# A fused recurrent and mixture-of-experts layer on 8 cores: the order of its tail and of its last weight loads

## The reference, cut to what matters

```
xn = layernorm(x)                                # x: 2 x 8192 tokens x 1024
h_t = sigmoid(A) * h_(t-1) + xn_t @ B            # 64 states, scan over time
s  = h @ C + xn @ D
r  = sigmoid(xn @ gate_w + gate_b)               # 16 experts, the best 2 per token
mlp(x, wg, wu, wd) = (silu(x @ wg) * (x @ wu)) @ wd      # 1024 -> 512 -> 1024
moe = w1 * mlp(xn, expert_1) + w2 * mlp(xn, expert_2)    # w1 + w2 = 1
out = x + s * silu(xn + mlp(xn, shared) + moe)
```

## Time and profile before

| | us |
|---|---|
| median of 3 timed runs | 740.28 (739.29 to 740.67) |
| the profiled execution | 733.69 |
| span of its slowest core (core 6) | 732.1 |
| spans of the 8 cores | 721.0 to 732.1 |
| PE / VectorE / ScalarE / GpSimd busy on the page's core (span 731.9) | 454.5 / 245.6 / 176.1 / 163.6 |

### The profile page before, as it was taken

How to read it: one execution, slowest core, us unless ns; L and a number is a source line. 1 busy time by engine, 2 the same in 40 slices (tenths; PEclk the granted TensorE clock), 3 DMA queues, 4 the chain that set the end, 5 groups by cost and what they waited for, 6 DMA issues and landing times.

```text
span 731.9 us, 7940 instructions; the slowest of 8 cores (721.0 to 732.1 us)
## 1 busy us (share of the span) xinstructions
PE 454.5 (62%) x2742; PEld 246.0 (34%) x2776; DVE 245.6 (34%) x437; ACT 176.1 (24%) x242; POOL 163.6 (22%) x167
## 2 busy tenths in 40 slices
PE   0126649965995484782872975838838787874530
PEld 0123324433552252450540543515514333331210
DVE  3763533472211121120210211201202567772235
ACT  0233321301322131320320321313203132221111
POOL 2110110022332132141230331412202123231113
PEclk9999968999999698797896997988979899997785
DMA  8971129401999999999999999999997565663421
GB/s 191 235 249 58 45 100 159 87 27 56 154 179 198 186 213 173 194 199 199 183 194 203 189 164 204 199 190 165 197 207 213 191 220 197 217 213 124 169 109 57
DMA packets 29705, 122.71 MB, mean 168 GB/s; under 512 B 5277, under 2 KB 5661, under 8 KB 22880
## 3 DMA queue, kind: packets, MB, share of 16 engines
q0 software_dynamic: 17136, 81.15, 58.7%
q1 hardware_dynamic: 12528, 41.03, 16.3%
HBM read 150.87 MB, written 33.55 MB: 252 GB/s over the span
## 4 chain that ended last, share of the span: by engine, by line
DMA 33%; PE 31%; DVE 14%; ACT 7%; issue 6%; DVEq 4%; POOL 2%; POOLq 1%; SPq 0%; ACTq 0%
DMA y_dram<-ysb,pidx 25%; PE ps L764 10%; PE ps L378 8%; PE ps L382 8%; DVEq L79 4%; DVE xgT L1085 4%; DVE xgT L1088 3%; DMA x_sb<-x_in 2%; ACT ysb L1091 2%; ACT xgT L1053 2%; DMA xn_dram<-xgT 2%; DMA a_t<-adiag 2%; PE ps L722 1%; POOL ysb L1095 1%; PE ps L466 1%
## 5 line engine op out<-in xcount | busy, mean ns | idle before, releaser
L764 PE MATMUL ps<-ring,xgT 128*128 128x512 bf16 (+1 forms) x368 | 101.0, 414 | 115.2 <-ACT ysb L775 89.3
L777 DVE COPY ysb<-ps 128x512 f32<-128x512 f32 (+1 forms) x48 | 33.1, 691 | 206.5 <-DMA y_dram<-ysb,pidx 120.9
L764 PEld LDWEIGHTS ps<-ring,xgT 128*128 128x128 bf16 (+1 forms) x384 | 36.7, 109 | 174.7 <-issue 152.0
L378 PE MATMUL ps<-xgT,ring 128*128 128x320 bf16 x512 | 82.2, 304 | 8.4 <-ACT silu L392 7.0
L382 PE MATMUL ps<-xgT,ring 128*128 128x320 bf16 x512 | 80.3, 300 | 0.0
L775 ACT ACTIVATE ysb<-ps 128x512 f32<-128x512 f32 (+1 forms) x48 | 28.6, 595 | 206.4 <-DMA y_dram<-ysb,pidx 135.2
L392 ACT ACTIVATE silu<-ps 128x320 f32<-128x320 f32 (+1 forms) x80 | 37.6, 470 | 136.2 <-PE ps L382 135.9
L399 DVE TENSOR_TENSOR xgT<-silu,ps 128x320 bf16<-128x320 f32 x64 | 31.2, 488 | 115.2 <-ACT silu L392 115.2
L1069 PE MATMUL ps<-ring,xnT 128*128 128x512 bf16 x252 | 67.2, 412 | 2.1 <-DVE ysb L1093 1.9
L1095 POOL TENSOR_TENSOR ysb<-ysb,x_sb 128x1024 f32<-128x1024 f32 x16 | 38.7, 2417 | 125.0 <-DVE ysb L1093 125.0
L378 PEld LDWEIGHTS ps<-xgT,ring 128*128 128x128 bf16 x512 | 48.5, 99 | 32.7 <-issue 14.5
(11 more groups left out here) (130 smaller groups left out, 471.1 us busy)
## 6 DMA issues: line engine op xcount, KB each, us to landing
ring<-ewg POOLq DMA_DIRECT2D x16, 1024.0 KB
ring<-ewu POOLq DMA_DIRECT2D x16, 1024.0 KB, 24.9
ring<-ewd POOLq DMA_DIRECT2D x16, 1024.0 KB, 23.6
ring<-y_dram SPq DMA_DIRECT2D x32, 512.0 KB, 5.4
x_sb<-x_in SPq DMA_DIRECT2D x16, 512.0 KB, 25.7
out<-ysb SPq DMA_DIRECT2D x16, 512.0 KB, 3.0
xn_dram<-xgT SPq DMA_DIRECT2D x16, 256.0 KB, 3.2
ysb<-x_in SPq DMA_DIRECT2D x6, 512.0 KB, 7.4
```

Of the source, the lines that this page charges most:

```text
L378: PE.op(lambda e, c=c: e.matmul(bank(p)[:, 0:n], slot_gu(m, c, ic), rhs(c), start=(c == 0), stop=(c == 7)))
L764: f = lambda q, k=k, h=h, dst=dst: q.matmul(dst, inter(e, k, o, n), slot_d(m, k, h), start=(k == 0), stop=(k == 3))
L777: k2 = V.sig(lambda q, to=to, src=src: q.tensor_copy(to, src))
```

## The change

The order of things changes in five places. The number of instructions of each kind and the bytes moved stay the same.

1. Loads 47, 48, 49 are now the shared down and D's halves; loads 50, 51, 52 are expert 15's gate, up and down. The `y_load` buffers move with them. When each numbered load is issued stays as it was.
2. `tail_front(0)` and the first sum of tile 0 stand between expert 15's gate and up and its down.
3. The first sum is taken out of `tail_front` (`tail_sum`); that of tile t+1 now stands between fma2 and the product of tile t.
4. x of tiles 12 to 15 is asked for in `tail_back(t)`, t = 0 to 3, right behind the write of tile t.
5. The part for overfull experts uses other PSUM banks and another buffer; it has nothing to do here.

```diff
+            if m >= M_SD and m < M_SD + 3:
+                return (swd, dmat[0], dmat[1])[m - M_SD]
+            e, j = divmod(m - 2, 3) if m < M_SD else (E - 1, m - M_SD - 3)
+            return (ewg, ewu, ewd)[j][e]
-        M_SD = 2 + 3 * E
+        M_SD = 2 + 3 * (E - 1)
+        def m_of(e):
+            return 2 + 3 * e if e < E - 1 else M_SD + 3
...
         for e in range(E):
-            m = 2 + 3 * e
+            m = m_of(e)
...
             for mm in (m + 6, m + 7):
-                if mm < M_SD + 3:
+                if mm < M_SD + 6:
                     load_w(mm)
...
+            if e == E - 1:
+                PE.wait(FREE_G[0], FREE_G[1], FREE_U[0], FREE_U[1], prev_scan[0],
+                        T_W[M_SD], T_W[M_D0], T_W[M_D1], *[T_MUL[("s", g)] for g in range(16)])
+                A.wait(FREE_XGT[e])
+                tail_front(0)
+                tail_sum(0)
             PE.wait(T_W[m + 2], *[T_MUL[(e, ic)] for ic in range(4)])
...
         def tail_front(t):
             b = 4 * (t % 2)
-            if t >= NXR:
-                s = t - NXR
-                SP.wait(T_F[s])
-                T_XR[t] = SP.dma(lambda e: e.dma_start(out=x_fin(t), in_=x_rows(t)), s_xr[s])
-            A.wait(T_XR.get(t), T_S.get(t - 2), LASTPE, T_DV)
+            A.wait(T_XR.get(t), T_S.get(t - 2))
...
-            V.wait(T_AN[t], T_P1[t])
-            T_A1[t] = V.sig(lambda e: e.tensor_tensor(ab[t % 2], ab[t % 2], bank(b, 2), ALU.add))
+        def tail_sum(t):
+            V.wait(T_AN[t], T_P1[t])
+            T_A1[t] = V.sig(lambda e: e.tensor_tensor(ab[t % 2], ab[t % 2], bank(4 * (t % 2), 2), ALU.add))
...
         def tail_back(t):
...
             T_S[t] = A.sig(lambda e: e.activation(g, a, AF.Silu))
+            if t + 1 < NT:
+                tail_sum(t + 1)
             V.wait(T_S[t], T_P2[t])
             T_H[t] = V.sig(lambda e: e.tensor_tensor(g, g, bank(b + 2, 2), ALU.mult))
...
             T_O[t] = SP.dma(lambda e: e.dma_start(out=out[t * 128:(t + 1) * 128, :], in_=g), s_o[t % 3])
+            if t + NXR < NT:
+                T_XR[t + NXR] = SP.dma(lambda e: e.dma_start(out=x_fin(t + NXR), in_=x_rows(t + NXR)), s_xr[t])
...
         for t in range(2):
             T_YF[t] = y_load(t)
-        tail_front(0)
+        PE.wait(T_DV, T_DA)
```

More of the change, by code:

```diff
@@ L753, in down_tile @@
         def down_tile(e, j, o, p0, n):
-            m = 4 + 3 * e
+            m = m_of(e) + 2
             yb = j % NYB
@@ L801, in build_nc, with x_fin @@
             FREE_Y[b] = R["inv"]
+        M_D0, M_D1 = M_SD + 1, M_SD + 2
+        XW = [slot(m_of(E - 1) + i) for i in range(3)]
+        yf = [w.bitcast(F32) for w in XW]
+        ab = [xgT[:, i * 2048:(i + 1) * 2048].bitcast(F32) for i in range(2)]
+        gb = [ysb[:, i * D:(i + 1) * D] for i in range(3)]
+        T_AN, T_P1, T_P2, T_A1, T_A2, T_A3, T_S, T_H, T_O, T_F = ({} for _ in range(10))
+        T_YF, T_XR = {}, {}
+        def x_fin(t):
+            s = t if t < NXR else t - NXR
+            return x_sb[:, s * D:(s + 1) * D]
@@ new lines, in y_load @@
+        def y_load(t):
+            SP.wait(T_DONE, *LASTG)
+            if t >= 3:
+                SP.wait(T_A3[t - 3])
+            SP.dma(lambda e: e.dma_start(out=yf[t % 3][:, 0:D],
+                                         in_=y_dram[t * 128:(t + 1) * 128, :]), s_yf[t % 3])
+            return SP.dma(lambda e: e.dma_start(out=yf[t % 3][:, D:2 * D],
+                                                in_=y_dram[T_OWN + t * 128:T_OWN + (t + 1) * 128, :]),
+                          s_yf[t % 3])
@@ new lines, in tail_front @@
+        def tail_front(t):
+            b = 4 * (t % 2)
+            A.wait(T_XR.get(t), T_S.get(t - 2))
+            T_AN[t] = A.sig(lambda e: e.activation(ab[t % 2], x_fin(t), AF.Identity,
+                                                   bias=nmr[:, t:t + 1], scale=rstd[:, t:t + 1]))
+            PE.wait(T_A1.get(t - 2))
+            for h in range(2):
+                for k in range(4):
+                    f = lambda e, h=h, k=k: e.matmul(bank(b + h), interS[:, k * T_OWN + t * 128:k * T_OWN + (t + 1) * 128],
+                                                     slot_d(M_SD, k, h), start=(k == 0), stop=(k == 3))
+                    if (h, k) == (1, 3):
+                        T_P1[t] = PE.sig(f)
+                    else:
+                        PE.op(f)
+            PE.wait(T_H.get(t - 2))
+            for h in range(2):
+                PE.op(lambda e, h=h: e.matmul(bank(b + 2 + h), hs[:, HALO + t * 128:HALO + (t + 1) * 128],
+                                              csb[:, h * 512:(h + 1) * 512], start=True, stop=False))
+                for c in range(8):
+                    f = lambda e, h=h, c=c: e.matmul(
+                        bank(b + 2 + h), xnT[:, c * T_OWN + t * 128:c * T_OWN + (t + 1) * 128],
+                        slot_d(M_D0 if c < 4 else M_D1, c % 4, h), start=False, stop=(c == 7))
+                    if (h, c) == (1, 7):
+                        T_P2[t] = PE.sig(f)
+                    else:
+                        PE.op(f)
@@ new lines, in tail_sum, with tail_back @@
+        def tail_sum(t):
+            V.wait(T_AN[t], T_P1[t])
+            T_A1[t] = V.sig(lambda e: e.tensor_tensor(ab[t % 2], ab[t % 2], bank(4 * (t % 2), 2), ALU.add))
+        def tail_back(t):
+            b = 4 * (t % 2)
+            a = ab[t % 2]
+            g = gb[t % 3]
+            V.wait(T_YF[t], R["w"])
+            V.drain()
+            V.op(lambda e: e.scalar_tensor_tensor(a, yf[t % 3][:, 0:D], wts[:, t:t + 1], a,
+                                                  ALU.mult, ALU.add))
+            V.drain()
+            T_A3[t] = V.sig(lambda e: e.scalar_tensor_tensor(a, yf[t % 3][:, D:2 * D], wts[:, NT + t:NT + t + 1],
+                                                             a, ALU.mult, ALU.add))
+            A.wait(T_A3[t], T_O.get(t - 3))
+            T_S[t] = A.sig(lambda e: e.activation(g, a, AF.Silu))
+            if t + 1 < NT:
+                tail_sum(t + 1)
+            V.wait(T_S[t], T_P2[t])
+            T_H[t] = V.sig(lambda e: e.tensor_tensor(g, g, bank(b + 2, 2), ALU.mult))
+            G.wait(T_H[t])
+            T_F[t] = G.sig(lambda e: e.tensor_tensor(g, g, x_fin(t), ALU.add))
+            SP.wait(T_F[t])
+            T_O[t] = SP.dma(lambda e: e.dma_start(out=out[t * 128:(t + 1) * 128, :], in_=g), s_o[t % 3])
+            if t + NXR < NT:
+                T_XR[t + NXR] = SP.dma(lambda e: e.dma_start(out=x_fin(t + NXR), in_=x_rows(t + NXR)), s_xr[t])
@@ L834, in build_nc @@
             FREE_W[m + 2] = FREE_INT[e] = k
-            if m + 8 < M_SD + 3:
+            if m + 8 < M_SD + 6:
                 load_w(m + 8)
@@ L838, in build_nc @@
                 scatter(j)
-        XW = [ring[:, s * 4096:(s + 1) * 4096] for s in ((2 + 3 * 15) % NRING, (3 + 3 * 15) % NRING,
-                                                         (4 + 3 * 15) % NRING)]
         fx = xg[:, 0:D]
-        fxT = xgT[:, 0:1024]
+        fxT = xgT[:, 5120:6144]
         fin = xgT[:, inter0:inter0 + 512]
@@ L878, in pe_extra @@
                                 o = c * 512 + ic * 128
-                                k = e.matmul(bank(2 * w)[:, ic * 128:(ic + 1) * 128], XW[w][:, o:o + 128],
+                                k = e.matmul(bank((7, 5)[w])[:, ic * 128:(ic + 1) * 128], XW[w][:, o:o + 128],
                                              fxT[:, c * 128:(c + 1) * 128], start=(c == 0), stop=(c == 7))
@@ L897, in act_extra @@
                     e.sem_inc(f_gu.h, -1)
-                    e.activation(fsil, bank(0), AF.Silu).then_inc(f_s.h, 1)
+                    e.activation(fsil, bank(7), AF.Silu).then_inc(f_s.h, 1)
         def dve_extra(e):
@@ L950, in dve_extra @@
                     e.sem_inc(f_s.h, -1)
-                    e.tensor_tensor(fin, fsil, bank(2), ALU.mult).then_inc(f_i.h, 1)
+                    e.tensor_tensor(fin, fsil, bank(5), ALU.mult).then_inc(f_i.h, 1)
                     e.wait_ge(f_y.h, 1)
@@ L1079, in tail_back @@
[L1079 to L1097, removed]
```

## The result

| | before | after |
|---|---|---|
| median of 4 timed runs, us | 739.78 | 714.17 (713.07 to 717.0) |
| ratio to before, 95% interval | | 0.969 (0.965 to 0.972) |
| profiled execution / its slowest span | 733.69 / 732.1 | 715.22 / 713.7 |
| fma1 of tile 0, mean over 8 cores (latest core) | 571.0 (576.4) | 588.4 (595.2) |
| fma1 of tile 0 to fma1 of tile 15 | 142.3 to 143.7 | 105.8 to 106.9 |

The change makes the kernel 25.6 us faster by the medians, 23 by the ratio; 719.5 was forecast, 20.8 us less than before. The last two lines of the table are read from each core's timeline. They show the change as a loss of 17.4 us ahead of the tail (mean) and a gain of 37 in it. The difference, 19.5 us, is near that of the profiled executions (18.5); why the medians lie further apart is taken up at the end.

A forecast was written before the change was run, and what follows sets the result against it. Experts held by the weight-load queue, the tail by a VectorE-ScalarE ring with late x stalls; tail start 15.9 us later (8.3 + 2.0 + 5.6), tail 36.7 shorter: 740.28 - 20.8 = 719.5 us, range 711 to 728.

The forecast's parts named there:

- Early x: Tail, tiles 11 to 14: requesting x earlier removes the stalls, some 33 of the 36.7 us gain; request cost taken as 0.
- (d): Measured interval, not a forecast term: fma1 of tile 0 to fma1 of tile 15; mean 143.0 us before, 106.1 after.
- First sum ahead of the product: Tail step on VectorE: 7.25 us against 7.42, because GpSimd's addition and the two fma take turns; naive step 6.2.
- Late weights: Expert 15's first up group waits for its up weights, load 51, landing at 554.9: 8.3 us later on core 6.
- (a): Measured interval: start of expert 14's last part of down to expert 15's first up group; mean 4.7 us before, 14.4 after.
- Clock: PE in expert 15 after idling for loads: a phase at 1.2 GHz costs 2.0 us, between 0 and 2.8.
- First products ahead of the down: Tile 0's 26 products on PE, now ahead of expert 15's down and not covered by anything: 5.6 us later.
- (c): Measured interval: expert 15's down to fma1 of tile 0; mean 20.4 us before, 19.3 after.
- (b): Measured interval: expert 15's first up group to its down; mean 9.1 us before, 17.3 after.
- the faster one (no turn-taking): Rival for the tail: the addition only slows one fma, step 6.2 us, 15 us less, 704.5 us; chance 0.10.
- the slower outcome: Rival: PE falls to 1.2 GHz in the tail and stays; 4 us per such tile, 775 at 14 tiles; chance 0.03.
- The transfers: Rival, early tail: x, y and writes together delay four tiles by 2 us each, 727.5 us; chance 0.07.

The follow-up runs named there:

- the run with the clock held: Changed kernel plus 28 unused products on PE, around expert 15's first gate group where PE waits for loads; 710.66 us, 0.966 of the kernel before.
- the runs with steps near 5.3 us: Changed kernel with GpSimd's addition waiting for the next tile's fma2, 684.08 us; that plus old load order, first products behind the down, x requests spread out, 671.44 us.

## Why the prediction was right

Point by point, by the steps of the prediction:

- **Early x** (33 us): right. 32.9 us by itself, (d) 32.6. On SP it added its own issue (0.42 us); in the changed kernel x landed in 5.1 to 5.4 us each on core 1, with fma1 steps of 7.14 to 7.20 beside it. Cores 4 and 5 have single steps of 7.7 to 8.8 us between tiles 3 and 6; over all cores (d) varies by 1.1 us, where up to 2 us for each of four tiles had been allowed.
- **First sum ahead of the product** (step 7.25, not 6.2): right. Steps of 7.13 to 7.20, fma2 3.21, addition 3.44. The tail was forecast at 106.7 from fma1 0 to fma1 15, it is 105.8 to 106.9. The 2.09 us of fma1 in the earlier trace rows, read in the prediction as mere slowing, fit turns too: the addition ends at 591.05, 1.01 us into fma1, and 1.08 us are left, near fma1's 1.28.
- **Late weights** (8.3 us of wait): the mechanism right, the size right for late cores and low for the others. (a) grew by 9.6 us on average, from 7.8 on cores 1 and 7 to 12.3 on core 5. The landing of one load from core 6, then the slowest, stood for all cores. Of the rival that has these weights land 6 us later, this is a part, but not on the cores that set the time: from the four latest cores of before (1, 2, 5, 6) to the four latest of after (1, 3, 4, 7), (a) grew by 7.9. By its own sign for core 6 (first up group at 555, wrong if before 550; fma1 0 at 592) the prediction missed: there it is 548.8 and 585.8, because core 6 was among the early cores in this execution. On core 1, now the slowest, they are 557.6 and 595.2.
- **Clock** (2.0): 2.1 by the run with the clock held.
- **First products ahead of the down** (5.6): 6.1 with the 0.35 of their later start.
- **Left out:** on the early cores the last part of expert 15's down no longer waits for a scatter behind the load queue. (c) is 19.3 in place of 20.4 on average, a gain of 1.1 us; it is 20.0 to 21.6 in all runs with the old load order and 19.3 to 19.6 in the others. From the down to the last scatter it took 8.7 to 10.4 us on cores 0, 3, 4 and 7 before, and 7.5 on cores 1, 2 and 6; after, 7.5 to 7.6 on all. So the latest cores gained nothing: (c) is 19.9 before and 19.8 after on them. That this is the scatter's wait was read from the timelines, not tried by itself.
- **Sum:** start of the tail 15.9 later was forecast; it is 17.4 on average, and 18.8 from latest core to latest core. From the four latest cores to the four latest, (a), (b) and (c) give 7.9 + 8.3 - 0.1 = 16.1; expert 14's last part of down, ahead of all that the change was costed for, starts 1.0 us later, and its cause is open. The profiled execution, forecast at 712.9, took 715.2.
- **From the profiled execution to the median:** here the forecast erred most. I carried over that the median stood 6.6 us above the profiled execution. After the change the profiled execution lies among the timed ones (715.22; 713.07 to 717.0). The profiled execution of before (733.69) was merely faster than all of its timed ones (736.8 to 740.67); why, no run shows. The two errors, 2.3 us low and 7.6 us high, leave 719.5 against 714.2. That they have opposite signs is luck; the terms of the sum do not depend on it.

Of the rivals, the faster one (no turn-taking) fell by the row of fma2. The clock did fall in the tail for one phase after tile 0 and recovered, as in the earlier trace rows; the slower outcome had nothing behind it. The transfers became a limit only in the runs with steps near 5.3 us.

## What to carry to other kernels

A stall in an in-order issue list is worth more than any reordering behind it: one request moved gave 33 us, while the two moves made around it to fill time (work ahead of the last expert's down, and the loads that this work needed) cost 15 to 17. Before work is moved ahead of something, ask what the thing behind it releases; here a chain of scatter, landing and reload that nothing covered. And when two engines take turns at a resource, place their work by which operations share it: a wait of 3 us on GpSimd gave 22 to 24 us.

## What the runs showed of the hardware

- VectorE's operations with two SBUF operands and GpSimd's addition take turns as whole instructions: 1.28 + 2.2 + 1.28 us, in every tile from 1 on and on every core of the changed kernel. Products and sums with one operand in PSUM run beside the addition at their full 1.22 us, and the addition takes its 2.37 there. The Trainium skill (SBUF — State Buffer, "Who interferes with whom") says that a VectorE instruction with two SBUF inputs contends with a GpSimd instruction that reads SBUF, and one with at most one SBUF input does not; the rows agree with both.
- Each core's place in the field changes from execution to execution: cores 0, 3, 4 and 7 were some 10 us ahead of the others in the profiled execution before, cores 0, 2, 5 and 6 after it, by 5 to 13 us. A forecast from one core's landing times holds for that core's place: the growth of (a) ran from 7.8 to 12.3 us.
